# An attention output projection cut into four row tiles of TensorE, with the engine orders changed around it

## What is computed

```python
xn = layernorm(x)
out = x + attention(xn) + moe(xn)
# attention: q, k, v = xn @ (basis @ coeffs.T), 32 channels each; no softmax
#   scores[t, s] = (q_t . k_s) * decay ** max(s - t - 1, 0) * (s > t)
#   attention = (scores @ v) @ o_w.T * out_scale          # the o-projection, 32 -> 128
# moe: top 2 of 4 experts, softmax of their logits
#   e0 = (silu(xn @ w1) * (xn @ w3)) @ w2                  # 128 -> 512 -> 128
#   e1 = gelu(linear(xn) ...) @ c2w + c2b                  # 128 -> 256 -> 128
#   e2 = layernorm(h2 + relu(h2 @ f1) @ f2 ...) @ gen_w    # 128 -> 256 -> 128
#   e3 = gelu(xn @ ml_w1 + b) @ ml_w2 + b                  # 128 -> 512 -> 128
```

## Time and profile before

| | us |
|---|---|
| median of 3 runs (456.71 to 459.86) | 456.83 |
| the profiled execution | 456.72 |
| its span on the core | 454.9 |
| TensorE (PE) busy | 443.0 |
| VectorE (DVE) busy | 404.0 |
| ScalarE (ACT) busy | 269.6 |
| GpSimd (POOL) busy | 250.3 |

### The profile page before, as it was taken

One profiled execution on the slowest core, in us unless ns is written; L12 is line 12 of the kernel. 1 busy time (PEld: TensorE's weight loads), 2 busy tenths in 40 slices (PEclk: granted clock), 3 DMA queues, 4 the chain that ended last, 5 costly groups with the idle time before them and its releaser, 6 DMA issues.

```text
span 454.9 us, 9548 instructions
## 1 busy us (share of the span) xinstructions
PE 443.0 (97%) x2788; PEld 369.3 (81%) x2788; DVE 404.0 (89%) x1327; ACT 269.6 (59%) x534; POOL 250.3 (55%) x366
## 2 busy tenths in 40 slices
PE   4999999999999999999999999999999999999996
PEld 4778788888878878888888878888887887888776
DVE  5788989989999899899989998998999989998897
ACT  4864828466383855838475482846738385583840
POOL 3883727557273674727457372765727367471551
PEclk9999999999999999999999999999999999999999
DMA  7522123041222303123040312303122230311101
GB/s 262 32 71 71 24 71 69 25 101 39 64 54 69 69 23 92 24 77 61 26 109 26 85 30 69 69 23 98 40 64 51 65 73 23 92 25 53 19 0 48
DMA packets 86483, 27.18 MB, mean 60 GB/s; under 512 B 64992, under 2 KB 82112, under 8 KB 86464
## 3 DMA queue, kind: packets, MB, share of 16 engines
q1 hardware_dynamic: 86176, 26.94, 24.6%
q10 hardware_dynamic: 288, 0.01, 0.0%
HBM read 14.66 MB, written 12.06 MB: 59 GB/s over the span
## 4 chain that ended last, share of the span: by engine, by line
issue 47%; POOL 38%; POOLq 11%; DVE 1%; DMA 1%; PE 1%; SPq 0%; ACT 0%; DVEq 0%
POOL hid3l L480 15%; POOL hidl L484 9%; POOLq L446 7%; POOL n L448 6%; POOL xn L448 5%; POOLq L493 2%; POOLq L440 2%; POOL WL L465 1%; POOL rstd_u L494 1%; DMA W<-weights 1%; PE S L966 1%; POOL negmean_c L439 1%; POOL negmean_x L439 0%; POOLq L134 0%; DVE OUT L939 0%
## 5 line engine op out<-in xcount | busy, mean ns | idle before, releaser
L1088 PE MATMUL S<-xh,WH 128*128 128x512 f32 x224 | 98.8, 441 | 0.2 <-DVE gate L803 0.2
L1090 PE MATMUL S<-xh,WL 128*128 128x512 f32 x224 | 88.6, 396 | 0.0
L1089 PE MATMUL S<-xl,WH 128*128 128x512 f32 x224 | 88.3, 394 | 0.0
L480 POOL TENSOR_TENSOR hid3l<-hid,hid3h 128x512 fp32r<-128x512 f32 x64 | 80.3, 1288 | 0.0
L438 POOL TENSOR_TENSOR veps_x<-mv_x,eps 128x4 f32<-128x4 f32 x16 | 3.2, 200 | 120.0 <-DVE mv_x L635 120.0
L1028 PEld LDWEIGHTS EX<-scaled,hid 128*128 128x128 f32 x512 | 59.5, 192 | 2.3 <-issue 1.0
L1028 PE MATMUL EX<-scaled,hid 128*128 128x128 f32 x512 | 59.8, 275 | 0.6 <-issue 0.6
L613 ACT ACTIVATE hid<-S,me_b 128x512 f32<-128x512 f32 x32 | 22.0, 687 | 61.6 <-PE S L1090 61.4
L1088 PEld LDWEIGHTS S<-xh,WH 128*128 128x128 f32 x224 | 42.2, 188 | 17.2 <-issue 3.6
L803 DVE SCALAR_TENSOR_TENSOR gate<-th,S 128x512 f32<-128x512 f32 x64 | 43.9, 686 | 8.2 <-ACT th L559 7.4
L1089 PEld LDWEIGHTS S<-xl,WH 128*128 128x128 f32 x224 | 42.3, 189 | 10.2 <-issue 3.6
(11 more groups left out here) (185 smaller groups left out, 1062.5 us busy)
## 6 DMA issues: line engine op xcount, KB each, us to landing
X<-x SPq DMA_DIRECT2D x16, 256.0 KB, 2.8
turning<-xn SPq DMA_DIRECT2D x15, 256.0 KB, 2.0
xb<-turning SPq DMA_DIRECT2D x60, 64.0 KB, 2.5
turning<-e3T SPq DMA_DIRECT2D x15, 256.0 KB, 2.4
e3b<-turning SPq DMA_DIRECT2D x60, 64.0 KB, 2.5
out<-OUT SPq DMA_DIRECT2D x15, 256.0 KB, 2.4
W<-weights SPq DMA_DIRECT2D x1, 768.0 KB, 8.3
W<-weights SPq DMA_DIRECT2D x1, 512.0 KB, 5.9
```

The source lines that it names most:

```text
L480: pool.tensor_tensor(hid3l[:, j, :], hid[3][:, j, :], hid3h[:, j, :], ALU.subtract) \
L1088: pe.matmul(bank[:, :], wh, hi, start=True, stop=False)
L1089: pe.matmul(bank[:, :], wh, lo, start=False, stop=False)
L1090: pe.matmul(bank[:, :], wl, hi, start=False, stop=True).then_inc(unit_ready, 1)
```

## The change

The o-projection becomes four products, one for each token tile: 32 partitions of `found` against the same 32 partitions of `back`, which is now 128 by 128 with the projection in each strip. The four go to four different banks: tiles 2 and 3 to two new units `o2` and `o3`, tile 0 to ATT, tile 1 to TR, for which TensorE first waits until 9 steps of the routing chain are done. VectorE adds the input tile by tile, in four instructions of 128 columns, `o2` and `o3` first. UNITS has 26 names in place of 24. Orders that change with it:

- TensorE: the transposes of `n1` before `sc`; `st` behind gates(1); `f1_0` and `f1_1` before expert 2; `m0` and `m1` before expert 0. In the first turn fold_first behind gates(0), fold_last directly behind fold_second.
- VectorE: `u_combine` and expert 0's addition earlier; `turn_next` directly behind the additions; `expert2_scale` behind silu(2); the transpose of `e3b` before silu(3); `coef` behind silu(3); the bias addition before `u` instead of behind it. In the first turn fold_first before silu(0), fold_last before the o additions, turn_next behind silu(3).
- ScalarE: tanh of `lean` and half_gate(2) before the copy of `hidh`. GpSimd: the clearing of `back` (line 428) goes.

```diff
-UNITS = ["tok0", "tok1", "tok2", "tok3", "a0", "b0", "c0", "c1", "c2", "c3", "sc", "st",
-         "a1", "b1", "f1_0", "f1_1", "a2", "b2", "a3", "b3", "e3", "f2", "m0", "m1"]
+UNITS = ["tok0", "tok1", "tok2", "tok3", "a0", "b0", "c0", "c1", "c2", "c3", "sc", "a1",
+         "b1", "st", "f1_0", "f1_1", "o2", "o3", "a2", "b2", "a3", "b3", "e3", "f2", "m0", "m1"]
-        back = sb("back", [NT * C, T])
+        back = sb("back", [NT * C, P])
-            const(pool.memset(back[:, :], 0.0))
-                act.copy(back[t * C:(t + 1) * C, t * P:(t + 1) * P], oT[:, :]).then_inc(back_laid, 1)
+                act.copy(back[t * C:(t + 1) * C, :], oT[:, :]).then_inc(back_laid, 1)
...
# ScalarE
-                act.wait_ge(released[g.bank("f1_1")], g.uses_before("f1_1") + 1)
-                act.copy(hidh[:, :, :], hid[2][:, :, :]).then_inc(hid_high, 1)
                 act.wait_ge(lean_ready, g.count(1, 1))
                 act.activation(tlean[:, :, :], lean[:, :, :], ACT.Tanh).then_inc(tlean_ready, 1)
                 half_gate(2)
+                act.wait_ge(released[g.bank("f1_1")], g.uses_before("f1_1") + 1)
+                act.copy(hidh[:, :, :], hid[2][:, :, :]).then_inc(hid_high, 1)
                 half_gate(3)
...
# VectorE
+                if first:
+                    fold_first()
                 silu(0)
+                if not first:
+                    u_combine(g.prev())
...
+                if not first:
+                    expert0(g.prev())
...
-                if first:
-                    fold_first()
-                if not first:
-                    expert0(g.prev())
-                if not first:
-                    u_combine(g.prev())
...
+                if first:
+                    fold_last()
+                wait(dve, out_stored[g.par], g.half(DMA_INC, 0))
+                for t in (2, 3):
+                    o, free = unit(f"o{t}")
+                    dve.tensor_tensor(OUT[g.par][:, t, :], o[:, 0:P], X[g.par][:, t, :], ALU.add).then_inc(free, 1)
+                dve.wait_ge(att_ready, g.count(1, 1))
+                for t, o in ((0, ATT[:, 0, :]), (1, TR[:, 0:P])):
+                    ins = dve.tensor_tensor(OUT[g.par][:, t, :], o, X[g.par][:, t, :], ALU.add)
+                ins.then_inc(att_added, 1)
+                if not first and not last:
+                    turn_next(g)
+                silu(2)
                 if not first:
                     expert2_scale(g.prev())
-                wait(dve, out_stored[g.par], g.half(DMA_INC, 0))
-                dve.wait_ge(att_ready, g.count(1, 1))
-                dve.tensor_tensor(OUT[g.par][:, :, :], ATT[:, :, :], X[g.par][:, :, :], ALU.add) \
-                    .then_inc(att_added, 1)
-                silu(2)
-                if not first and not last:
-                    turn_next(g)
...
-                f2, free = unit("f2")
-                dve.scalar_tensor_tensor(out=u[:, :], in0=f2[:, :], scalar=vec("f2b"), in1=h2[:, :],
-                                         op0=ALU.add, op1=ALU.add).then_inc(free, 1)
                 dve.wait_ge(att_added, g.count(1, 1))
                 for t in range(NT):
                     ins = dve.scalar_tensor_tensor(out=OUT[g.par][:, t, :], in0=row("me_c2b"),
...
                 ins.then_inc(bias1_added, 1)
+                f2, free = unit("f2")
+                dve.scalar_tensor_tensor(out=u[:, :], in0=f2[:, :], scalar=vec("f2b"), in1=h2[:, :],
+                                         op0=ALU.add, op1=ALU.add).then_inc(free, 1)
...
# TensorE
                 if first:
                     fold_second()
                 if not first:
                     expert1(g.prev())
+                if first:
+                    fold_last()
...
                 pe.wait_ge(found_taken, g.count(1, 1))
-                pe.matmul(qk_bank, found[:, :], back[:, :], start=True, stop=True).then_inc(att_ready, 1)
-                if first:
-                    fold_last()
+                pe.wait_ge(route_step, g.count(ROUTE_STEPS, ROUTE_STEPS - 1))
+                banks = [fill("o2"), fill("o3"), ATT[:, 0, :], TR]
+                for t, bank in zip((2, 3, 0, 1), banks):
+                    rows_ = slice(t * C, (t + 1) * C)
+                    ins = pe.matmul(bank[:, 0:P], found[rows_, :], back[rows_, :], start=True, stop=True)
+                    if t in (2, 3):
+                        ins.then_inc(unit_ready, 1)
+                ins.then_inc(att_ready, 1)
                 gates(2)
...
+                if first:
+                    pe.wait_ge(setup_took, len(TAKEN))
+                three("m0", SPLIT["me"], h, l)
+                three("m1", SPLIT["me"] + P, h, l)
                 if not last:
...
                     expert0(g)
-                if first:
-                    pe.wait_ge(setup_took, len(TAKEN))
-                three("m0", SPLIT["me"], h, l)
-                three("m1", SPLIT["me"] + P, h, l)
```

More of the change, by code:

```diff
@@ L783, in turn_next @@
                 dve.wait_ge(h2_ready, g.count(1, 1))
+                dve.wait_ge(att_added, g.count(1, 1))
                 dve.wait_ge(x_swapped, g.count(SWAPS * DMA_INC, SWAPS * DMA_INC))
@@ L900, in turn @@
                         .then_inc(ex_ready[3], 1)
+                silu(3)
+                if first:
+                    turn_next(g)
+                dve.wait_ge(tlean_ready, g.count(1, 1))
+                route(dve.scalar_tensor_tensor(out=coef[g.par][:, :, :], in0=tlean[:, :, :], scalar=1.0,
+                                               in1=half[:, :, :], op0=ALU.add, op1=ALU.mult))
                 if not first:
@@ L1119, in turn @@
                     three(f"c{j}", SPLIT["ml"] + j * P, h, l)
+                for t in range(NT):
+                    pe.wait_ge(c_normed, g.count(NT, t + 1))
+                    ins = pe.transpose(TR[:, t * P:(t + 1) * P], n1[:, t, :], ident[:, :])
+                ins.then_inc(c_turned, 1)
                 pe.wait_ge(qk_split, g.count(1, 1))
@@ L1125, in turn @@
                 ins.then_inc(unit_ready, 1)
[L1126 to L1129, removed]
+                gates(1)
                 pe.wait_ge(kd_ready, g.count(1, 1))
@@ L1135, in turn @@
                 ins.then_inc(unit_ready, 1)
-                gates(1)
                 if first:
@@ L1151, in turn @@
                 ins.then_inc(found_ready, 1)
-                if not first:
-                    expert2(g.prev())
                 pe.wait_ge(h2_low, g.count(1, 1))
@@ L1156, in turn @@
                 three("f1_1", SPLIT["f1"] + P, h2h[:, :], h2l[:, :])
+                if not first:
+                    expert2(g.prev())
                 if first:
@@ L1214 @@
 IDLE_BEHIND = 3
-POOL_CONSTS = 11
+POOL_CONSTS = 10
 ACT_SETUP = 4
```

## The result

The changed kernel takes 462.85 us (median of 4 runs) against 456.77 us: a ratio of 1.0106, 95% interval 1.0075 to 1.0136. It is slower by 1.1 to 1.3%, where I forecast 1.5 us, 0.3%, faster and called slower by more than 1% unlikely (0.14). The time lies outside the range of 450.0 to 460.0.

What follows compares the result with a forecast made beforehand. TensorE's own work was taken to set the turn. 15 turns x 0.235 us saved (-3.5), first turn +0.6 and last turn +1.4 gave -1.5 us, from 456.72 to 455.2, range 450.0 to 460.0.

Steps and rivals of the forecast that it cites:

- What bounds the kernel: Ordinary turns: TensorE's own work sets the 27.05 us; VectorE costs nothing while some 0.45 us of cover remain.
- Its wait for o2: VectorE, ordinary turn: waits 0.2 us for the split o-projection's tiles after finishing expert 1.
- The o-projection: TensorE, each turn: four row tiles cost 0.63 us in place of 0.865, a gain of 0.235; block 0.98 us.
- without drain: Rival at the o-projection: row tiles need no pause, gaining 0.55 to 0.64 a turn; 449.8 to 450.5 us, chance 0.15.
- with loads in a queue: Rival at the o-projection: eight wide loads pass one by one, 465 us, chance 0.09; milder form 460, chance 0.09.
- the load rule of the Trainium skill: O-projection weights: load time goes by columns, not rows, so a 32 by 128 load costs as much as a full one.
- the four moves: TensorE's reorderings move blocks without adding any, so they change nothing: 0, give or take 0.05 us a turn.
- The first turn: Later gates(2) costs +1.3 us, partly regained where m0 and m1 cover expert 0's wait: net +0.6 us.
- The wait for me2: First turn, TensorE before fold_last: would arrive some 2 us before VectorE has me2, at 25.22, and wait.
- The last turn: u comes later behind the bias addition, slower o additions and expert2_scale: +1.4 us, and that turn's 0.235 gain lost.
- The sum: Whole kernel: 15 turns of 0.235 saved, -3.5; first turn +0.6; last turn +1.4; together -1.5 us.
- The rival that the gain is used up: VectorE or the routing wait becomes the bound, turns stay at about 27.0: 457 to 459 us, chance 0.12.

Runs made afterwards that it cites:

- e1: The kernel before with only the o-projection split into four products and four additions, other orders kept: 457.0 us against 456.95, ratio 0.9998.
- e2: The changed kernel with the o-projection as one product and one addition again, all changed orders kept: 465.25 us against 456.95 for the kernel before.
- e3: The changed kernel with the scores before the transposes of n1 and u_combine behind K's split again: 458.54 us against 456.95 for the kernel before.
- e9: The kernel before with one edit, the transposes of n1 ahead of the scores: 461.6 us against 456.80, ratio 1.0103.
- e8: The changed kernel with scores first, u_combine and fold_last back, first-turn tile 1 in EX[0], u before the bias addition: 455.17 us against 456.84 for the kernel before.
- e10: As e8, with fold_first also in its old place on TensorE and VectorE: 453.87 us against 456.80 for the kernel before.
- e7: The changed kernel with eight idle products on TensorE before fold_last in the first turn: 460.22 us against 456.84 for the kernel before.
- e4: The changed kernel with fold_last back behind the o-projection, first turn only: 461.1 us against 456.95 for the kernel before.
- e5: The kernel before with the split alone and tile 1 of the first turn in EX[0] instead of TR: 455.75 us against 456.84.
- s executions: Profiled executions, of whichever kernel, marked s because their first products ran at half pace; estimated to cost about 3 us.

## Why the prediction was wrong

**What bounds the kernel: right.** TensorE's own work sets the turn in both kernels, and VectorE never became the bound: it is busy for 24.93 of 27.08 us, and its wait for the transposes of u, which I had at 0.45, is 0.42 on average (5.5 us over 13 turns). Its wait for o2 is 0.46 where I wrote 0.2; it costs nothing there.

**The o-projection: right.** 0.97 us of block against 0.98, a gain of 0.23 (e1 against before, at the block) to 0.24 a turn (e2 against changed). It pauses on entering and leaving; its loads overlap. The rivals without drain and with loads in a queue are out. So is the load rule of the Trainium skill ("TensorE: Matmul & The Clock Gate", LDWEIGHTS) as an objection: a 32 by 128 load does take a wide load's time here (0.18 to 0.19 in its record), but four of them start within 0.02 us.

**"I put the four moves at 0, give or take 0.05 a turn": the step that failed.** It counted instructions, loads and mode changes, and these do cancel: `st` moved for nothing. But the order had a second function: the scores covered the end of GpSimd's normalisation. The row was in the trace: n1 done at 236.9 us, the first transpose at 236.82 and the fourth at about 237.15, 0.25 us of cover, less than the 0.42 by which the move brought the transposes forward. I looked for the waits that the change added by name and for banks, and not at each existing wait whose cover was moved. It cost 0.22 (e3) to 0.28 (e9) a turn: 3 to 4 us in all. None of my rivals had this wait.

**The first turn: right in kind, too small.** +0.6 was forecast, +2.75 came. The wait for me2 was 1.6 where I wrote "some 2 us"; me2 itself came 0.57 us later (25.79 for 25.22), 0.13 of it because the router started later and the rest since fold_first now stands before silu(0) on VectorE (0.46 between e8 and e10); and the half clock, which no term held, cost 1.5 (e7). 0.6 + 0.57 + 1.5 = 2.7.

**The last turn: right in kind, too large.** +1.4 forecast, +0.8 came by the trace; the wait for u was 1.77 us (1.5 to 2 expected), 1.27 more than before.

**The sum.** By its own terms, corrected: 14 turns of -0.24 and +0.29 give +0.7 (0.9 with the second turn's rest), first +2.75, last +0.8: +4.4, the span's 4.5. Of the 6 us between this and my -1.5, the ordinary turns are 4.4, the first 2.1 and the last -0.6. The rival that the gain is used up with turns near 27.0, at 457 to 459, came nearest; but it named VectorE or the routing wait as the cause, and it was GpSimd, with 27.10.

**Open.** With the split, c3 and the scores wait longer in every second turn (26.99 and 26.85 in e1, 26.95 and 26.81 in e3 and e10). UNITS of 26 names puts each unit two banks further in every second group, where 24 kept them; that is the one thing I know of that alternates, but I haven't tried another length. It holds back 0.14 us in every second turn, 0.07 on average, of the 0.235.

## What to carry to other kernels

Before an instruction block is moved ahead of another on the bounding engine, take the finish time of every operand it waits for and compare it with its new start; blocks of equal cost are not interchangeable when one covers a third engine. A split into 32-row tiles pays 0.4 us of pauses and an exposed load here, so by these rows it gains only where the product it replaces costs well over 0.6 us. A wait of 1.6 to 2.4 us on TensorE in the first turn could have a second price behind it in the clock; idle products in it, or better another order, give that back. Whether it is paid can differ between executions of one kernel (half of e1's), so read it from the granted clock.

## What the runs showed of the hardware that I had not expected

The clock fell after a single wait of 1.61 us, with TensorE busy for 5.95 of the 7.90 us up to the end of that wait: 0.54 granted in 26.8 to 30.5 us. After a wait of 1.6 us that idle products filled it was 1.00. After e4's wait of 2.07 us it was 1.00 too, and so it was behind the changed kernel's own 1.77 us in the last turn. The kernel before waits at most 0.64 us inside its first turn and has 1.00 there.

The start differs from execution to execution. In the profile of e8 the first products of the router run at half pace, 0.21 us apart in place of 0.11, and products of 512 columns 0.42 apart up to 19.4 us and 0.23 from there (timeline of TensorE).

```profile
14.90 0.42 PE L1106 MATMUL S<-TL,xh 128*128 128x196 f32 x1
15.11 0.42 PE L1107 MATMUL S<-TH,xl 128*128 128x196 f32 x1
...
19.00 0.58 PE L1093 MATMUL S<-xl,WH 128*128 128x512 f32 x1
19.42 0.39 PE L1094 MATMUL S<-xh,WL 128*128 128x512 f32 x1
19.65 0.39 PE L1092 MATMUL S<-xh,WH 128*128 128x512 f32 x1
```

The granted clock of 14.0 to 18.5 us is given as 1.00 there, but that is no reading: the clock record in e8's trace begins at 19.40 us, where the pace changes, and a stretch without a record is given as 1.00. In e7 it begins at 15.04, and the pace changes between 15.03 and 15.16; in the kernel before it begins at 9.95, ahead of the router, which runs at full pace. So the first stretch of the s executions ran at the lower level, 1.2 GHz, unseen in the column. My estimate is that it costs about 3 us: e8's transposes of u in the first turn stand 2.7 us behind e5's (43.23 for 40.49), and its profiled execution of 457.26 us lies 3.6 above its two fastest.

This fits the groups in the times (453.2, 454.5, 456.4 for e10; 456.6 and 459.9 for the kernel before): the profiled executions of e8, e9 and e10 with the slow start are in the upper group of their kernels, those of e5 and the kernel before with the full pace in the lowest. The middle group was never profiled. It is why differences of 1 us between medians of few runs settle nothing here.
